# Attention ahead of the third batch's slot products, and other homes for the halves of the expert weights

## What is computed

```python
x = L0_attn_x                                        # (4, 512, 256)
# attention: 16 heads of 16, rotated by head index, causal
scores = where(causal, q @ k.T, -inf)
attn   = softmax(scores) * 256 ** -0.5
x = layernorm(x + (attn @ v) @ w_proj + b_proj)
# experts: 8, the best 2 of each token
probs  = softmax(x @ router_w.T)
top_w, top_i = top_k(probs, 2); top_w /= sum(top_w)
for e in range(8):
    h   = silu(x @ ws[e, :512].T) * (x @ ws[e, 512:].T)
    out = out + combine[:, e:e+1] * (h @ w2s[e].T)   # combine: top_w, scattered by top_i
x = layernorm(x + out)
```

## Time and profile before

| what | value |
|---|---|
| median of 3 runs | 524.72 us (523.14 to 526.04) |
| the profiled execution | 526.1 us |
| its span on the core | 524.2 us, so 1.9 us lie around it |
| TensorE busy in the span | 444.0 us (85%) |
| VectorE, ScalarE, GpSimd busy | 309.1, 275.6, 229.2 us |
| mean granted TensorE clock | 0.935 of full speed |

### The profile page before, as it was taken

How to read it: one execution, slowest core, us unless ns; L and a number is a source line. 1 busy time by engine, 2 the same in 40 slices (tenths; PEclk the granted TensorE clock), 3 DMA queues, 4 the chain that set the end, 5 groups by cost and what they waited for, 6 DMA issues and landing times.

```text
span 524.2 us, 9270 instructions
## 1 busy us (share of the span) xinstructions
PE 444.0 (85%) x2920; PEld 271.1 (52%) x2920; DVE 309.1 (59%) x1095; ACT 275.6 (53%) x394; POOL 229.2 (44%) x314
## 2 busy tenths in 40 slices
PE   1999589899998799879947799999999999999800
PEld 0555224445554455445624567666766666667500
DVE  6185898677869977997688434565223223223224
ACT  0476349897876658765978234532332333333215
POOL 0000021112666557664836475545565555654322
PEclk9999759899989999999987799999999999999955
DMA  8378899222237423522321014343433323333254
GB/s 270 66 196 244 261 364 383 80 61 61 62 98 225 141 61 87 150 67 83 117 85 27 14 31 92 80 63 51 62 45 57 55 48 61 51 52 50 31 174 158
DMA packets 32976, 57.23 MB, mean 109 GB/s; under 512 B 5025, under 2 KB 23585, under 8 KB 31394
## 3 DMA queue, kind: packets, MB, share of 16 engines
q1 hardware_dynamic: 18306, 39.60, 24.1%
q0 software_dynamic: 7488, 10.27, 12.7%
q10 hardware_dynamic: 7136, 6.77, 4.2%
HBM read 38.64 MB, written 17.97 MB: 108 GB/s over the span
## 4 chain that ended last, share of the span: by engine, by line
PE 58%; DVE 20%; ACT 10%; DMA 5%; issue 4%; POOL 1%; SPq 1%; ACTq 0%; DVEq 0%; POOLq 0%
PE PS L1393 19%; PE PS L1420 12%; DVE PS L890 8%; PE PS L1229 5%; PE PS L1190 4%; PE PS L1412 3%; PE PS L1264 3%; PE PS L1211 2%; ACT PT L729 2%; PE PS L420 2%; PE PS L1385 2%; DMA qk_parts<-W 1%; DMA sum_rows<-PT,IDXA 1%; PE PS L1283 1%; DVE MX L890 1%
## 5 line engine op out<-in xcount | busy, mean ns | idle before, releaser
L890 DVE CUSTOM_DVE_ANT_0 PS<-PS,CB 128x512 f32<-128x512 f32 (+3 forms) x256 | 121.2, 516 | 31.3 <-PE PS L1190 30.3
L1393 PE MATMUL PS<-W,PT 128*128 x468 | 114.9, 382 | 3.2 <-issue 3.2
L729 ACT ACTIVATE PT<-PS 128x1024 f32<-128x1024 f32 x80 | 81.3, 1021 | 34.4 <-PE PS L1212 33.8
L687 POOL DMA_INDIRECT sum_rows<-PT,IDXA x39 | 62.1, 1592 | 70.8 <-ACT PT L849 64.0
L1190 PE MATMUL PS<-KQ 96*128 96x512 bf16 (+3 forms) x256 | 67.2, 330 | 16.4 <-DVE MX L890 10.9
L1148 DVE SCALAR_TENSOR_TENSOR PT<-PS,CW,PT 128x512 f32<-128x512 f32 x39 | 29.3, 750 | 68.3 <-ACT PT L842 68.3
L1393 PEld LDWEIGHTS PS<-W,PT 128*128 128x128 f16 x468 | 44.4, 98 | 42.4 <-issue 5.5
L1211 PE MATMUL PS<-KQ 104*128 104x512 bf16 (+3 forms) x256 | 62.0, 313 | 1.1 <-ACT PT L729 1.1
L1154 DVE COPY PT<-PS 128x512 f32<-128x512 f32 x39 | 27.0, 691 | 52.2 <-PE PS L1412 52.2
L838 ACT ACTIVATE PT<-PS 128x512 f16<-128x512 f16 x39 | 23.3, 597 | 65.5 <-PE PS L1385 65.5
L586 POOL TENSOR_SCALAR NM<-MX 128x16 f32<-128x16 f32 x16 | 4.8, 299 | 119.7 <-DVE MX L890 119.4
(11 more groups left out here) (186 smaller groups left out, 747.1 us busy)
## 6 DMA issues: line engine op xcount, KB each, us to landing
W<-w1T SPq DMA_DIRECT2D x8, 1024.0 KB, 14.2
qk_parts<-W SPq DMA_DIRECT2D x32, 192.0 KB, 3.1
KQ<-qk_parts SPq DMA_DIRECT2D x32, 192.0 KB, 2.9
KQ<-qk_parts SPq DMA_DIRECT2D x64, 64.0 KB, 3.0
x_rows<-X1S ACTq DMA_DIRECT2D x4, 516.0 KB, 3.5
W<-xT SPq DMA_DIRECT2D x4, 512.0 KB, 7.1
KQ<-qk_parts SPq DMA_DIRECT2D x16, 128.0 KB, 2.9
sum_rows<-X ACTq DMA_DIRECT2D x4, 512.0 KB, 3.1
```

Of the source, the lines that this page charges most:

```text
L687: pool.indirect_dma_start(acc_dram, bass.IndirectOffsetOnAxis(ap=IDXA[:, j, 0:1], axis=0), YS[j % TRIO], None, compute_op=ALU.add).then_in ...
L729: act.activation(PT[n][:, :], STb[slot_of(k, n)].rearrange("p a n -> p (a n)"), ACT.Exp).then_inc(s["exp"], 1)
L890: last = dve.tensor_tensor_reduce(src, src, maskS[:, TT * P - w:], 1.0, LOW, ALU.add, ALU.max, MX[p][:, h, i:i + 1])
L1393: last = mm(dst, XGT[j % TRIO][:, x_part, k, :], w1h[:, bass.ds(at, UNIT)], start=(k == x_part == w_part == 0), stop=(k == KC - 1 and x_pa ...
```

## The change

Three edits of the same stretch, all in tables; no function changes.

1. END_SLOTS_AT goes from (1, 3) to (1, 5), behind the transpose of the outputs and one more group of transposed scores; parts 17 and 18 go from (1, 4) to (1, 6); slot_values go from the end of step (4, 0) to position (1, 1).
2. The high halves move: 18 from (0, 7) to (0, 6), 20 from (0, 9) to (1, 1), and all later ones back by one to a few places; five stand in a row behind the last outputs, where three did.
3. GpSimd makes the low halves of 16, 20 and 25 instead of 16, 18 and 22. VectorE makes 18, 19, 22 to 24 at earlier or other places.

```diff
-        END_..., END_SLOTS_AT, END_ROWS_AT = (0, 5), (0, 6), (0, 9), (1, 3), (0, 9)
-        END_VALUES_AT = (0, 9)
-        END_ROUTE_AT = {..., (1, 4): (17, 18)}
+        END_..., END_SLOTS_AT, END_ROWS_AT = (0, 5), (0, 6), (0, 9), (1, 5), (0, 9)
+        END_VALUES_AT = (1, 1)
+        END_ROUTE_AT = {..., (1, 6): (17, 18)}
...
-                    (4, 0): (16, 18), (4, 1): (22,)}
+                    (4, 0): (16,), (4, 1): (20, 25)}
```

More of the change, by code:

```diff
@@ L469, in block_kernel @@
         X1_HIGH_AT, STORE_AT, ROWS_AT = (3, 9), (0, 5), (1, 6)
-        END_GATE_AT, END_RANKS_AT, END_COUNT_AT, END_SLOTS_AT, END_ROWS_AT = (0, 5), (0, 6), (0, 9), (1, 3), (0, 9)
-        END_VALUES_AT = (0, 9)
-        END_ROUTE_AT = {(0, 2): (0, 1), (0, 3): (2, 3), (0, 4): (4, 5), (0, 6): (6, 7), (0, 7): (8, 9), (0, 8): (10, 11, 12, 13, 14), (1, 4): (17, 18)}
+        END_GATE_AT, END_RANKS_AT, END_COUNT_AT, END_SLOTS_AT, END_ROWS_AT = (0, 5), (0, 6), (0, 9), (1, 5), (0, 9)
+        END_VALUES_AT = (1, 1)
+        END_ROUTE_AT = {(0, 2): (0, 1), (0, 3): (2, 3), (0, 4): (4, 5), (0, 6): (6, 7), (0, 7): (8, 9), (0, 8): (10, 11, 12, 13, 14), (1, 6): (17, 18)}
         HIGH_AT = {(2, 0, 1): 0, (2, 0, 5): 1, (2, 1, 1): 2, (2, 1, 5): 3, (2, 2, 1): 4, (2, 2, 6): 5, (2, 3, 1): 6, (2, 3, 5): 7,
                    (3, 0, 1): 8, (3, 0, 5): 9, (3, 1, 1): 10, (3, 1, 5): 11, (3, 2, 1): 12, (3, 2, 6): 13, (3, 3, 1): 14, (3, 3, 5): 15,
[2 rows of a table removed]
[2 rows of a table added]
         POOL_LOW = {(2, 0): (0, 1), (2, 1): (2, 3), (2, 2): (4,), (2, 3): (6,), (3, 0): (8, 9), (3, 1): (10, 11), (3, 2): (12,), (3, 3): (14,),
-                    (4, 0): (16, 18), (4, 1): (22,)}
+                    (4, 0): (16,), (4, 1): (20, 25)}
         POOL_UNITS = sum(POOL_LOW.values(), ())
-        LOW_AT = {(2, 2, 7): (5,), (2, 3, 7): (7,), (3, 2, 7): (13,), (3, 3, 7): (15,), (4, 0, 5): (17,), (4, 1, 1): (19, 20, 21),
-                  (4, 1, 6): (23, 24, 25), (4, 1, 8): (26, 27), (4, 2, 1): (28,), (4, 2, 5): (29, 30, 31)}
+        LOW_AT = {(2, 2, 7): (5,), (2, 3, 7): (7,), (3, 2, 7): (13,), (3, 3, 7): (15,), (4, 0, 5): (17,), (4, 0, 7): (18,), (4, 0, 8): (19,),
+                  (4, 1, 1): (21,), (4, 1, 5): (22, 23), (4, 1, 6): (24,), (4, 1, 8): (26,), (4, 2, 1): (27, 28), (4, 2, 5): (29, 30, 31)}
         def on_pool(u):
```

## The result

| | before | with the change |
|---|---|---|
| median of 22 runs each | 523.52 us | 521.39 us |
| ratio to before | | 0.9963, 95% interval 0.9947 to 0.9979 |
| span of the profiled execution | 524.2 us | 518.9 us |

The kernel is 1.9 us faster (0.0037 x 523.5), with an interval of 1.1 to 2.8; a gain of 2.0 was predicted. The time itself was put at 522.7, from a median of three runs of 524.72. The 521.39 is close to rival B's 521.2 for this reason alone: the gain is that of the forecast A.

The account below looks back on a forecast made before the run. Tiles are bound by TensorE, so only the first gate's start and the clock behind it count: 1.0 plus 1.0 us, sum 2.0, off the three-run median 524.72 gives 522.7 us; range 520.2 to 526.2.

Parts of the forecast that it names:

- rival B: Picks without the 1.07 us behind the decode, early table not lengthened: gate 1.0 to 2.0 sooner, about 521.2 us; 25%.
- forecast A: GpSimd's picks, gather and the row transposes end last, gate at 290.3, clock rises earlier: 522.7 us; 45%.
- What ends last: GpSimd's low 25 delays picks, gather (284.8) and row transposes (288.05); VectorE's last low half is done at about 286.4.
- The read of the expert's number at nothing: Ahead of the gate, the 1.10 us read runs beside the output transposes and is taken at 0.
- The gate: On TensorE, the first gate starts at 290.3 instead of 291.3, a gain of 1.0 us.
- The clock: Low-clock work behind the gate shrinks from 4.3 us to 1.5 to 3.6, giving 0.3 to 1.4; 1.0 taken.
- Start of step (4, 1): VectorE's low 18 moves the tables from 264.41 to 265.64; ScalarE's first exponentials come at 266.0 instead of 272.57.
- the wait that I had put ahead of high half 23: On ScalarE, high 23 waits for VectorE's low 21, which stands behind the early table, until 274.9.
- The decode: VectorE's decode takes 2.2 us instead of 3.0 without GpSimd's difference beside it, ending at 279.0.
- VectorE beside GpSimd: VectorE's low 24 inside GpSimd's scaling for unit 25 is charged nothing; beside the residual, low 31 had taken 2.98 us.
- rival C: VectorE's low 24 waits for GpSimd's scaling until 280.2, GpSimd's difference 0.6 late; gain 1.4, 523.3 us; 12%.
- Rival D: VectorE holds GpSimd's scaling of unit 25 by 2.07 us; gate 1.1 later than before, 525.6 us; 15%.

Follow-up runs that it names:

- the order alone: The kernel before with slots, decode and scalings at their new places, the halves at their old ones; ratio 1.0025 to the kernel before.

## Why the prediction was right

**What ends last.** The mechanism was right, and nearly every size. The step that carried it is the one that walks the change past GpSimd's queue: low 25 stands ahead of the picks, ends at 20.3 from H, gather at 23.7 and transposes at 26.9, measured 20.28, 23.60 and 26.87. The two runs that lengthened one queue each showed the same thing from both sides.

**The read of the expert's number at nothing.** Right: the earlier trace rows had 2.81 of idle ahead of the gate, and there is none now. In the order alone, where the halves end last again, the gate again comes 1.1 behind the last low half (30.12 and 31.23 from H). That the time is the read of the number is my reading of the code; no row names it.

**The gate.** Predicted 1.0 sooner, measured 1.23. The output transposes were put from 288.4 to 290.3, where the gate really begins at the issue of its first matmul, 0.2 before the modelled end of the last transpose (287.15, and 285.44 + 1.91).

**The clock.** Put at 1.0 with ends of 0.3 and 1.4; measured 0.68. The rise came 4.94 us behind TensorE's last gap (285.06 to 290.00), later than the 3.7 behind the last gap and the 4.3 behind the gate's start from which the 1.0 was taken, and inside the 1.5 allowed beyond them. The two gains came out at 1.9 for 2.0, so part of the agreement is luck: 0.2 more at the gate, 0.3 less from the clock. The rises in the experiments scatter by as much as is worth 1 us, so a forecast closer than that is luck too.

**Start of step (4, 1).** A term missed: the exponentials came at 5.49, not 4.9, for the 0.59 in ScalarE's row above. Low 18 ahead of part 10 of the routing delays its running counts (MRUN) too, and the count on TensorE (line 1354) waits for them (0.75 at 262.84) ahead of the first scores of the step. I had followed that wait to the row store alone. It went on to the scalings and the exponentials behind them, and was taken up by the wait that I had put ahead of high half 23. That half started at 13.77 from H, 13.8 predicted, but right behind the exponentials: VectorE's low 21 had ended 0.1 before.

**The decode.** Put at 2.2 without GpSimd's difference beside it, and it took 273.74 to 275.92, 2.18. The early table ran 0.24 better than put; one of its operations was held for 1.26 again, beside GpSimd's difference for unit 20.

**VectorE beside GpSimd.** Partly wrong. I charged nothing for low 24 beside a scaling. VectorE:

```profile
275.81 1.09 DVE L1027 SCALAR_TENSOR_TENSOR W<-W,SW 128x512 f16<-128x512 f32 x1
277.69 1.33 DVE L1027 SCALAR_TENSOR_TENSOR W<-W,SW 128x512 f16<-128x512 f32 x1 [0.79 <-ACT W L779]
```

The first is low 24. It began 0.2 behind the start of the scaling of 1.63 and took 0.34 longer than its 0.75. The second is low 26. It began 0.4 behind the start of the difference, which ended at 278.47, and ended 0.55 after it. So the rival C happened in small: low 24 was held a little, not until the scaling was over, and GpSimd's work was not pushed back. The rule of the Trainium skill (SBUF — State Buffer, Who interferes with whom), by which the second to start blocks fully, fits the second row and not the first. Nor does the row at 287.23, which the prediction took to agree, show the order that the rule asks for: low 31 began 0.06 us ahead of the residual and was held all the same. In the order alone the case is clearer, with the residual from 288.25 for 2.37 and VectorE's low 30 at:

```profile
287.93 3.25 DVE L1027 SCALAR_TENSOR_TENSOR W<-W,SW 128x512 f16<-128x512 f32 x1
```

It began 0.3 ahead of the residual and ended 0.56 behind it. By the recorded starts, being first did not help VectorE; the profile gives GpSimd's spans roughly, so this is a hint and not proof.

Rival D did not come: the scaling took 1.63, not 3.64. Rival B's early picks did not come either: 0.99 stood between low 25 and the first pick.

## What to carry to other kernels

Ask of each in-order queue what stands ahead of the instruction that starts the next stage. Here one low half of 2.8 us on an engine that was 44% busy stood ahead of three picks and cost 2 us of the 4 that the change could have given; the share of busy time does not show that. And judge a reordering with all its tables: each of the two parts of this change, the order and the places of the weight halves, made the kernel slower when it came alone, by 0.25% and 0.27%. In both, ScalarE met other waits instead (2.94 for low 19; 2.13 for the tables and 1.66 for low 22).

## What the runs showed of the hardware

- The granted clock rose from 0.50 to 1.00 between 3.2 us (292.94 to 296.17, the order alone, where it had fallen only at 292.76) and 5.4 us (285.24 to 290.60, above) behind TensorE's last gap. At half speed for the work in between, this spread is worth 1 us, nearly as much as the whole move of the gate (1.23); it turned a loss of 1.90 into 1.03 and a gain of 0.8 into a loss of 0.5.
- A two-input operation of GpSimd (a difference or the residual) held VectorE instructions with two SBUF inputs until its end each time: 1.26 for 0.29 in the early table, and eight low halves that ended 0.54 to 0.56 behind it. It held a cast with one input as well (1.08, 0.25 in the changed kernel). A one-input scaling held a low half by 0.34 at most, or not at all (0.75).
- A scaling of GpSimd that began 0.3 us into four tables of VectorE took 3.64 us in one trace and 2.35 in another, for 1.57 beside a single low half.
